# Another order of the attention stage's 100 steps per group

## The chip, the cores and the metric

One core of a Trainium2 chip runs the whole kernel. The metric is the device time of one launch in microseconds, as the median of several runs.

## What is computed

A macaron layer on x of 2 x 1024 x 256 in float32: half a feed-forward block, attention, half a feed-forward block again, each with a layer norm before it.

```
x = x + 0.5 * ffn(layernorm(x))     # silu(x Wg) * (x Wu), 2 of every 4 kept by size, times Wd; hidden 1024
x = x + attention(layernorm(x))     # 32 heads of 8, 8 heads of keys and values, rotary, causal, softmax
x = x + 0.5 * ffn(layernorm(x))
```

The change is in the attention alone:

```
scores = q k^T / sqrt(8), masked above the diagonal      # 1024 x 1024 for each head
attn   = softmax(scores)                                 # with the row's maximum taken off first
out    = attn v, then out Wo + bo
```

## The kernel before

The kernel has four phases: feed-forward, the projections to q, k and v, attention, feed-forward. Each engine has its own program, and semaphores tie them together. The attention works through 16 **groups**: 2 sequences times 8 key heads, with the 4 query heads that share a key head. The maximum of each row of scores is needed before the exponentials. So the scores are computed twice: once with queries on the partitions, for the maxima (`maximum_scores`, L1325), and once with keys on the partitions, for the exponentials (`s_head`, L1354). In the second, the maxima are taken off by rows that are added to q.

Per group there are four kinds of steps, and TensorE, ScalarE and GpSimd all take them in the order of one string, `ORDER`:

- **m**, 48 of them: one matmul of 64 rows, 128, 256, 384 or 512 columns wide, into one of four banks (`m_ps`). VectorE takes the maximum of each (L1418 with the causal mask, L1421 without), in the same sequence. The first 32 m's of the string are of the second half of the next group's rows, the last 16 of the first half of the group after. They alternate wide and narrow: m0 to m7 are 512 and 128 columns, m8 to m15 512 and 256, m16 to m23 512 and 384, m24 to m32 all 512, then m33 128 and m34 512, and on to m39 128 and 512 in turns, m40 to m47 384 and 256. After m31 VectorE joins the maxima of the two halves of the keys (L1436).
- **s**, 40 of them: one head of a unit of scores, into one of three banks (`s_ps`). ScalarE takes the exponential (L1471) into one of five buffers (`probs`). A unit is four heads. The string's s's run two units ahead of its v's. s's take their operands from partitions 0 to 63, m's from 64 to 127 (`s_lane`, `m_lane`).
- **t**, 2 of them: four transposes of the split maxima of 512 rows, into a bank of `m_ps` (`turn_shift`, L1333). ScalarE copies it out (L1477), and SP loads it by four DMAs into q (L1594). GpSimd makes the split (L1533, L1535) from VectorE's maxima.
- **v**, 10 of them: one unit of probabilities times values, for four heads, into one bank (`o_ps`, L1370). Units 0, 3 to 7 are 512 columns wide, 1 and 8 are 256, 2 and 9 are a piece of 384 and one of 128. Units 0, 1, 2 and 7, 8, 9 lie on the diagonal, and GpSimd masks them first (L1510). After v2 and v9 ScalarE copies the bank out (L1484), and v3 and the next v0 wait for that.

An m waits for VectorE to be done with the user of its bank, an s for the exponential three heads back, a v for the exponentials and masks of its unit. Banks of m's and t's are dealt in turns along the order:

```
RING = first_steps + [step for g in range(GROUPS) for step in steps(g) if step[0] in "mt"]
BANK = {step: i % M_BANKS for i, step in enumerate(RING)}
BANK_USER = dict(zip(RING[M_BANKS:], RING))
```

VectorE has other work in some groups: in groups 10 and 14 four reciprocals each (L1078), between m's. In groups 14 and 15 the m's run out.

Of the kernel before, what the change touches and what calls it, by code (L numbers as in the profile page):

```python
# [1164 lines left out]
def attention_programs(nc, ctx, group_rows, v, region, s_ps, m_ps, o_ps, output, normed, ident_bf, x, bo_row, T, HD, earlier):  # L1165
# [23 lines left out]
    for qc in range(QC):  # L1189
# [31 lines left out]

    ORDER = ("msmssmvsmmmsmsvsmmsmtmsmmmssmsmvs"
             "mmmssmsmvsmsmmsvmssmmsvmsmsmsvmsm"
             "ssmmsssmvssmmmtmsvmmmssmsmvmsmssmm")
    FIRST_MAXIMA = 16
    FIRST_TURNS = (26, 11)
    LEAD_IN = 1
    FIRST_HEADS = (AHEAD + LEAD_IN) * QPK  # L1230
    assert [ORDER.count(kind) for kind in "smtv"] == [SU * QPK, MU, QC, SU]

    def steps(g):

        count = dict.fromkeys("smtv", 0)
        for kind in ORDER:
            n = count[kind]
# [430 lines left out]
def build(nc, x_in, w_qkv, bias_cols, bv, w_o, bo, w_gate, w_up, w_down, cos_t, sin_t, out, HD=8, SPLIT=4):  # L1668
# [7 lines left out]
    with ExitStack() as ctx:  # L1676
# [55 lines left out]
        for b in range(BLKS):  # L1732
# [24 lines left out]
        late = Region(nc, late_at)  # L1757
        output = Output(nc, ctx, late, hole, x, w_o.rearrange("(k p) n -> p k n", p=P), inverse_rows, KVH, C // HD // KVH, HD, T, N, out_ps)
        attention, before_groups, first_scores, first_maxima, hooks = attention_programs(
            nc, ctx, group_rows, v, att_region, s_ps, m_ps, o_ps, output, normed2, ident_bf, x, bo, T, HD, earlier)  # L1760
        between["fills"] += [lambda pool: group_rows.fill_q(pool, 0),
# [55 lines left out]
```

## Time and profile before

| | |
|---|---|
| median of 3 runs | 829.38 us (826.87 to 832.43) |
| the profiled execution | 832.21 us |
| its span | 830.7 us |
| TensorE busy | 774.4 us, 93% |
| VectorE busy | 721.2 us, 87% |
| ScalarE busy | 491.5 us, 59% |
| GpSimd busy | 262.3 us, 32% |
| attention's groups | from about 250 to 680 us |

Times in the rows are microseconds from the start of the span. The profile shows when each instruction ran on its engine, and the idle time before it in brackets with what ended it. Instructions of one line that follow each other are merged into one row, with their number behind an x; the time is that of all of them. TensorE's ends are modelled. PEclk is the share of TensorE's full clock that was granted.

### The profile page before, as it was taken

To read this page: it belongs to the slowest core of one execution; us is meant where nothing else is said; L and a number is where in the kernel's file an instruction comes from. 1 tells how busy PE (TensorE), PEld (TensorE's weight loads), DVE (VectorE), ACT (ScalarE), POOL (GpSimd) and SP (SyncE) were. 2 spreads that over 40 slices of the span, in tenths; PEclk is the share of its full clock that TensorE was granted. 3 is DMA by queue.
4 is the path that set the end of the run, shared out by engine and by line. 5 is a ranking of instruction groups with operands and counts; after the bars stand their busy time and mean duration, and the time that the engine had idled before them with its cause. 6 is when DMAs were issued, how large, how long until landed. Compare 5 with 4: busy or idle time off the path is not lost.

```text
span 830.7 us, 15658 instructions
## 1 busy us (share of the span) xinstructions
PE 774.4 (93%) x5168; PEld 508.7 (61%) x5168; DVE 721.2 (87%) x1862; ACT 491.5 (59%) x949; POOL 262.3 (32%) x359
## 2 busy tenths in 40 slices
PE   4999999989899999999999989999899999999996
PEld 3787887977654544444444444444444468888886
DVE  3989999986797999999999989999987259999997
ACT  6444443311135888888888868888678734443441
POOL 1143533058720332322322222155315210534330
PEclk9999999999857999999999989999999999999999
DMA  8100000026913321233311332533313000000001
GB/s 294 53 0 2 0 1 1 1 107 173 297 33 69 71 66 37 61 74 72 70 41 39 72 70 54 132 67 76 72 21 85 15 8 1 1 26 1 26 2 51
DMA packets 21968, 48.62 MB, mean 59 GB/s; under 512 B 3744, under 2 KB 8224, under 8 KB 21376
## 3 DMA queue, kind: packets, MB, share of 16 engines
q1 hardware_dynamic: 21824, 47.56, 21.9%
q8 instruction: 41, 0.67, 0.4%
q14 instruction: 39, 0.32, 0.1%
q10 hardware_dynamic: 64, 0.07, 0.0%
HBM read 19.63 MB, written 14.16 MB: 41 GB/s over the span
## 4 chain that ended last, share of the span: by engine, by line
PE 61%; DVE 20%; issue 8%; POOL 5%; ACT 5%; DMA 1%; PEldq 0%; DVEq 0%; PEld 0%; SPq 0%; ACTq 0%; POOLq 0%
PE att_o_ps L1370 17%; PE att_m_ps L1325 15%; PE att_s_ps L1354 10%; PE ffn_gate L218 5%; PE ffn_up L218 5%; PE ffn_y_ps L351 5%; DVE ffn_hs L524 2%; DVE ffn_h L566 2%; POOL qkv_turned L859 2%; POOL qkv_parts L864 2%; ACT att_probs L1471 2%; DVE att_maxima L1421 2%; DVE att_scratch L1418 1%; DVE ffn_rank L510 1%; DVE ffn_pair_max L498 1%
## 5 line engine op out<-in xcount | busy, mean ns | idle before, releaser
L1471 ACT ACTIVATE att_probs<-att_s_ps 128x512 f32<-128x512 f32 (+1 forms) x640 | 314.3, 558 | 92.4 <-PE att_s_ps L1354 90.4
L1325 PE MATMUL att_m_ps<-k,q 64*128 64x512 f32 (+3 forms) x768 | 240.9, 413 | 15.5 <-DVE att_maxima L1418 13.6
L1418 DVE CUSTOM_DVE_ANT_0 att_scratch<-att_m_ps,att_causal 128x512 bf16<-128x512 f32 (+3 forms) x512 | 234.3, 485 | 20.9 <-PE att_m_ps L1325 17.9
L1354 PE MATMUL att_s_ps<-q,k 64*128 64x512 f32 (+3 forms) x768 | 223.3, 392 | 3.9 <-ACT att_probs L1471 3.9
L1325 PEld LDWEIGHTS att_m_ps<-k,q 64*128 64x128 f32 x768 | 132.9, 196 | 105.2 <-DVE att_maxima L1418 57.4
L1421 DVE TENSOR_REDUCE att_maxima<-att_m_ps 128x1 f32<-128x512 f32 x256 | 175.9, 687 | 11.5 <-PE att_m_ps L1325 11.3
L1370 PE MATMUL att_o_ps<-att_probs,att_vs 128*32 128x512 f32 (+3 forms) x1536 | 161.4, 508 | 1.6 <-POOL att_probs L1510 1.6
L1510 POOL TENSOR_SCALAR_AFFINE_SELECT att_probs<-att_probs 128x512 f32<-128x512 f32 x128 | 79.9, 637 | 262.3 <-ACT att_probs L1471 262.3
L1354 PEld LDWEIGHTS att_s_ps<-q,k 64*128 64x128 f32 x768 | 122.5, 190 | 64.8 <-ACT att_probs L1471 62.0
L630 POOL TENSOR_TENSOR ffn_hs_lo<-ffn_hs,ffn_hs_hi 128x512 fp32r<-128x512 f32 x48 | 76.6, 1621 | 106.4 <-ACT ffn_hs_hi L427 106.4
L454 ACT ACTIVATE ffn_a<-ffn_h 128x512 f32<-128x512 f32 x64 | 40.5, 633 | 106.8 <-DVE ffn_h L566 106.8
L351 PE MATMUL ffn_y_ps<-wd_hi,ffn_hs_hi 128*128 128x256 f32 x256 | 73.8, 288 | 6.2 <-DVE x L554 2.7
L351 PE MATMUL ffn_y_ps<-wd_lo,ffn_hs_hi 128*128 128x256 f32 x256 | 73.0, 285 | 0.0
L351 PE MATMUL ffn_y_ps<-wd_hi,ffn_hs_lo 128*128 128x256 f32 x256 | 72.9, 285 | 0.0
L1370 PEld LDWEIGHTS att_o_ps<-att_probs,att_vs 128*32 128x32 f32 x1536 | 34.1, 110 | 56.4 <-issue 41.8
L566 DVE TENSOR_TENSOR ffn_h<-ffn_up,ffn_silu 128x512 f32<-128x512 f32 x64 | 43.6, 682 | 23.0 <-ACT ffn_silu L449 22.0
L218 PE MATMUL ffn_gate<-ffn_xt_hi,wg_hi 128*128 128x512 f32 x128 | 52.2, 408 | 3.6 <-DVE ffn_h L566 1.6
L351 PEld LDWEIGHTS ffn_y_ps<-wd_hi,ffn_hs_hi 128*128 128x128 f32 x256 | 49.4, 193 | 9.4 <-DVE x L554 2.9
L218 PE MATMUL ffn_gate<-ffn_xt_lo,wg_hi 128*128 128x512 f32 x128 | 50.8, 397 | 0.9 <-DVE ffn_xt_lo L199 0.9
L427 ACT ACTIVATE ffn_hs_hi<-ffn_hs 128x512 fp32r<-128x512 f32 x56 | 35.0, 632 | 27.0 <-DVE ffn_hs L524 27.0
L218 PE MATMUL ffn_gate<-ffn_xt_hi,wg_lo 128*128 128x512 f32 x128 | 50.9, 398 | 0.0
L218 PE MATMUL ffn_up<-ffn_xt_lo,wu_hi 128*128 128x512 f32 x128 | 50.7, 396 | 0.0
(114 smaller groups left out, 1166.8 us busy)
## 6 DMA issues: line engine op xcount, KB each, us to landing
q_rows<-qkv_parts SPq DMA_DIRECT2D x16, 512.0 KB, 4.6
q<-q_rows SPq DMA_DIRECT2D x16, 512.0 KB, 4.6
q<-q SPq DMA_DIRECT2D x16, 512.0 KB, 4.3
k_rows<-qkv_parts SPq DMA_DIRECT2D x8, 256.0 KB, 3.0
k<-k_rows SPq DMA_DIRECT2D x16, 128.0 KB, 5.2
k<-k SPq DMA_DIRECT2D x16, 128.0 KB, 4.3
q<-att_shift_t SPq DMA_DIRECT2D x128, 4.0 KB
out_num<-att_sums SPq DMA_DIRECT2D x128, 16.0 KB
```

Source lines behind the costliest of these rows:

```text
L218: last = pe.matmul(bank, w[w_part], xt[:, k, :], start=(k == 0 and n == 0), stop=(k == self.KT - 1 and n == 2))
L351: last = pe.matmul(y_ps[:, t, :], hp[:, blk, j, rows], wp[:, blk, j, :], start=(blk == 0 and j == 0 and m == 0 and t % 2 == 0), stop=(blk ...
L454: act.activation(a[:, blk, j, :], h[:, blk, j, :], ACT.Abs).then_inc(abs_ready, 1)
L566: dve.tensor_tensor(h[:, blk, j, :], gu[j % 2][1][:], silu[:, j % 2, :], ALU.mult).then_inc(h_ready, 1)
L630: pool.tensor_tensor(hs_lo[:, blk, j, :], hs[:, j, :], hs_hi[:, blk, j, :].bitcast(F32), ALU.subtract).then_inc(lo_ready, 1)
L1325: pe.matmul(m_ps[BANK["m", n]][:, :cols], q[g % 2][m_lane, h, t * P:(t + 1) * P], k[g % 2][m_lane, kc * N:kc * N + cols], start=True, stop ...
L1354: last = pe.matmul(s_ps[n % S_BANKS][:, at:at + w], k[g % 2][s_lane, kb * P:(kb + 1) * P], q[g % 2][s_lane, h, qc * N + q0:qc * N + q0 + w ...
L1370: last = pe.matmul(o_ps[32 * h:32 * (h + 1), q0:q0 + w], vs[g % 2][:, kb, :], probs[u % len(probs)][:, h, at:at + w], start=(u in CHUNK_FI ...
L1418: dve.tensor_tensor_reduce(out=scratch[bank][:, :n], in0=m_ps[bank][:, :n], in1=causal[:, N - n:], scale=1.0, scalar=LOWEST, op0=ALU.add, ...
L1421: dve.tensor_reduce(top_of, m_ps[bank][:, :n], mybir.AxisListType.X, ALU.max).then_inc(m_taken, 1)
L1471: act.activation(probs[u % len(probs)][:, h, SPAN[u]], s_ps[n % S_BANKS][:, SPAN[u]], ACT.Exp, scale=SCALE).then_inc(exp_done, 1)
L1510: pool.affine_select(out=blk, in_=blk, compare_op=ALU.is_ge, fill=0.0, base=0, pattern=[[0, QPK], [1, P]], channel_multiplier=-1).then_inc ...
```

## The change

Only the string `ORDER` changes. It has the same 100 letters in another sequence: 40 s, 48 m, 2 t, 10 v. All three engines that read it follow, and the banks are dealt anew along it.

```diff
-    ORDER = ("msmssmvsmmmsmsvsmmsmtmsmmmssmsmvs"
-             "mmmssmsmvsmsmmsvmssmmsvmsmsmsvmsm"
-             "ssmmsssmvssmmmtmsvmmmssmsmvmsmssmm")
+    ORDER = ("smsmmvmsmsmsmvsmmmssmsmmtssmsmvms"
+             "mssmmsmmvsmmssmvmsmsmsvmsmsmsvsms"
+             "smmmsssmvmsmsmsmmvtsmmmmmsssmvmsmsm")
```

Cut at the v's, with v0 ahead of the first cut and the string's end joined to its start, these are the stretches behind each v:

```
     before               after
v0   smmmsms              msmsmsm
v1   smmsmtmsmmmssmsm     smmmssmsmmtssmsm
v2   smmmssmsm            msmssmmsmm
v3   smsmms               smmssm
v4   mssmms               msmsms
v5   msmsms               msmsms
v6   msmssmmsssm          smssmmmsssm
v7   ssmmmtms             msmsmsmm
v8   mmmssmsm             tsmmmmmsssm
v9   msmssmmmsmssm        smsmsmsmm
```

## Rows read from the trace of the kernel before

**Rows 1.** Windows of one group; us, then each engine's busy time, clock, DMA.
```profile
408.34:433.82 25.48, 24.43 (x201) 12.08 (x200) 23.82 (x82) 21.31 (x45) 6.60 (x15) 1.00 0.28 63
486.22:515.23 29.01, 27.35 (x201) 12.93 (x200) 25.54 (x84) 21.19 (x45) 6.37 (x14) 0.88 0.19 41
593.85:622.86 29.01, 26.83 (x202) 13.15 (x201) 25.85 (x84) 21.31 (x45) 6.36 (x14) 0.88 0.20 41
```

**Rows 2.** VectorE's maxima by shape, six ordinary groups; busy us, mean ns.
```profile
L1421 DVE TENSOR_REDUCE att_maxima<-att_m_ps 128x1 f32<-128x512 f32 x97 | 66.7, 688 | 2.0 <-PE att_m_ps L1325 2.0
...
L1418 DVE CUSTOM_DVE_ANT_0 att_scratch<-att_m_ps,att_causal 128x384 bf16<-128x384 f32 x48 | 26.5, 553 | 2.6 <-PE att_m_ps L1325 2.3
...
L1418 DVE CUSTOM_DVE_ANT_0 att_scratch<-att_m_ps,att_causal 128x256 bf16<-128x256 f32 x48 | 20.0, 418 | 0.0
...
L1418 DVE CUSTOM_DVE_ANT_0 att_scratch<-att_m_ps,att_causal 128x128 bf16<-128x128 f32 x48 | 13.7, 286 | 5.3 <-PE att_m_ps L1325 4.6
```

**Rows 3.** VectorE's timeline, one ordinary group; start, length in us.
```profile
410.06 0.29 DVE L1418 CUSTOM_DVE_ANT_0 att_scratch<-att_m_ps,att_causal 128x128 bf16<-128x128 f32 x1 [0.45 <-PE att_m_ps L1325]
...
415.95 0.69 DVE L1421 TENSOR_REDUCE att_maxima<-att_m_ps 128x1 f32<-128x512 f32 x1 [0.17 <-PE att_m_ps L1325]
...
427.79 0.29 DVE L1418 CUSTOM_DVE_ANT_0 att_scratch<-att_m_ps,att_causal 128x128 bf16<-128x128 f32 x1 [0.33 <-PE att_m_ps L1325]
...
429.66 0.29 DVE L1418 CUSTOM_DVE_ANT_0 att_scratch<-att_m_ps,att_causal 128x128 bf16<-128x128 f32 x1
...
431.96 0.56 DVE L1418 CUSTOM_DVE_ANT_0 att_scratch<-att_m_ps,att_causal 128x384 bf16<-128x384 f32 x1 [0.33 <-PE att_m_ps L1325]
```

**Rows 4.** TensorE's timeline, the same group; ends are modelled.
```profile
410.28 0.64 PE L1370 MATMUL att_o_ps<-att_probs,att_vs 128*32 128x256 f32 x8
...
411.92 0.38 PE L1333 MATMUL att_m_ps<-ident_bf,att_shift 128*8 128x128 bf16 x4 [0.29 <-DVE att_maxima L1421]
...
412.23 0.49 PE L1325 MATMUL att_m_ps<-k,q 64*128 64x512 f32 x1
...
414.27 1.07 PE L1370 MATMUL att_o_ps<-att_probs,att_vs 128*32 128x384 f32 x16
...
417.12 1.06 PE L1370 MATMUL att_o_ps<-att_probs,att_vs 128*32 128x512 f32 x8
...
420.34 0.39 PE L1325 MATMUL att_m_ps<-k,q 64*128 64x512 f32 x1
...
420.57 0.39 PE L1325 MATMUL att_m_ps<-k,q 64*128 64x512 f32 x1
...
424.34 0.52 PE L1325 MATMUL att_m_ps<-k,q 64*128 64x512 f32 x2
...
425.78 1.07 PE L1370 MATMUL att_o_ps<-att_probs,att_vs 128*32 128x512 f32 x8
...
427.61 0.38 PE L1333 MATMUL att_m_ps<-ident_bf,att_shift 128*8 128x128 bf16 x4
...
428.14 0.49 PE L1325 MATMUL att_m_ps<-k,q 64*128 64x512 f32 x1 [0.15 <-DVE att_maxima L1418]
...
428.58 0.64 PE L1370 MATMUL att_o_ps<-att_probs,att_vs 128*32 128x256 f32 x8
...
429.15 0.33 PE L1325 MATMUL att_m_ps<-k,q 64*128 64x128 f32 x1
...
430.01 0.38 PE L1325 MATMUL att_m_ps<-k,q 64*128 64x256 f32 x1
...
430.33 1.07 PE L1370 MATMUL att_o_ps<-att_probs,att_vs 128*32 128x384 f32 x16
...
433.40 0.49 PE L1325 MATMUL att_m_ps<-k,q 64*128 64x512 f32 x1
```

**Rows 5.** Timelines of ScalarE and of SP's queue, the same group.
```profile
432.12 0.59 ACT L1484 ACTIVATE att_sums<-att_o_ps 128x512 f32<-128x512 f32 x1
...
429.04 2.40 SPq L1594 DMA_DIRECT2D q<-att_shift_t  x4
```

More of the change, by code:

```diff
@@ L1219, in attention_programs @@
     LAST = GROUPS - 1
-    ORDER = ("msmssmvsmmmsmsvsmmsmtmsmmmssmsmvs"
-             "mmmssmsmvsmsmmsvmssmmsvmsmsmsvmsm"
-             "ssmmsssmvssmmmtmsvmmmssmsmvmsmssmm")
+    ORDER = ("smsmmvmsmsmsmvsmmmssmsmmtssmsmvms"
+             "mssmmsmmvsmmssmvmsmsmsvmsmsmsvsms"
+             "smmmsssmvmsmsmsmmvtsmmmmmsssmvsmsm")
     FIRST_MAXIMA = 16
```

## The prediction

> **What bounds the kernel now.** I read the windows first, one per group of the attention stage, from a group's first value step to the next group's. An ordinary group lasts 25.48 us, and in it TensorE is busy 24.43, VectorE 23.82, ScalarE 21.31 [rows 1]. No engine is full and two nearly are. The change keeps every instruction and moves only places in a queue, so busy time stays and only idle time can go. Then I read VectorE's timeline: the gaps in rows 3 lie each at the first m behind a v. Last, TensorE's timeline, for what it was doing there.
>
> Names: m0 to m47, s0 to s39, T0, T1 and v0 to v9 are the letters of ORDER, counted by kind. v0 opens the window at 408.34 and the next v0 closes it at 433.82 [rows 1]; between them v1 is at 410.28, v2 414.27, v3 417.12, v7 425.78, v8 428.58, v9 430.33 [rows 4].
>
> **What the change leaves alone.** From v3 to v7 (8.66 us, [rows 4]) the new order has the same m's and s's between the same v's, some neighbours swapped: nothing. The last score of a unit stands 5 to 8 scores ahead of its v, as before, so exponentials and masks are in time. Nothing is added on POOL or SP. ScalarE's copy of the output bank behind v9 runs until 432.71, 2.38 us after v9 [rows 5]; my walk puts the next v0 2.72 after it, so it fits, by 0.3. T1 moves behind m39 and v8, and with it SP's four loads of the shift, issued in 2.40 us from 429.04, 1.43 after T1 at 427.61 [rows 4, 5]; next_m and store_sums stand behind them on SP, both early. s4 needs these loads. In my walk it comes 6.5 us after T1; 1.4 for the copy, 2.4 for the issue and 1.2 for the last landing (an estimate: half of the issue time) make 5.0. It fits by 1.5 us; each us beyond would cost a us per group.
>
> **The laws that I walk with.** (a) m's and T's share four banks in a ring. An m starts 0.07 after VectorE is done with the unit four places back (m38 at 428.14: m35 was started at 427.79 and took 0.29, [rows 3, 4]); a T in between counts as a place. (b) Units of 512, 384, 256 and 128 columns take 688, 553, 418 and 286 ns [rows 2]. 24 of the widest and 8 of each other make 26.6 us a group, 2.8 more than VectorE is busy [rows 1]: where there is no gap, a unit starts before the last one's end, by 2.8 over some 40 such places, 0.07; I take 0.08, so 0.61, 0.47, 0.34 and 0.20 from start to start. (c) What follows a v starts 0.07 before its end, 0.57 after v8 (m39 at 429.15), 1.0 after the longer ones. VectorE takes an m that is first behind a v 0.51 later (128 columns, m39, taken at 429.66) to 0.63 (384: v9 to m44, 1.63 in all), and one behind a score 0.1 to 0.2 later still (v0 to m3 1.72, v2 to m16 1.68) [rows 3, 4]. (d) From the last m to the v it is 0.42 (m2, 433.40), or 0.32 if that m is 256 wide (m43, 430.01) [rows 4].
>
> **The walk**, v7 as zero. Today s31 and s32 stand between v7 and m35; VectorE gets m35 2.01 after v7, having ended m34 0.33 before [rows 3]. In the new order m35 is first and VectorE takes it as soon as it can, 0.33 + 0.08 earlier, at 1.60.
> **v7 to v8**: m36 to m39 are taken at 1.80, 2.41, 2.61, 3.22. m39 waits for m35's bank (1.96), so v8 is at 2.20.
> **v8 to v9**: T1 at 2.77; T0 to m10 took 0.31 (411.92, 412.23, [rows 4]), so m40 starts at 3.08 and reaches VectorE at 3.71, which was free at 3.42. m41 is taken at 4.18 and done at 4.60, which gives m45 its bank at 4.67; v9 at 5.00. The units go on to 6.14.
> **v9 to v0**: s38 first, so m46 reaches VectorE at 5.00 + 1.68 = 6.68. m2 needs its bank: 6.68 + 0.55 + 0.07 = 7.30, v0 at 7.72.
> **v0 to v1**: m3 first, taken at 9.23; VectorE was free at 8.91. There are nine weights to load here for today's eight, so 2.05 for 1.94 and v1 at 9.77.
> **v1 to v2**: m7 stands behind s5 and comes at 11.05, 0.2 late. From there VectorE sets the pace, 0.20 + 0.61 + 0.34 + 0.61 to m11 at 12.81, done 13.23. And here the new order loses: T0 stands between m12 and m13, no longer between m9 and m10, so m14, the last m before v2, has m11's bank: m14 at 13.30, v2 at 13.72. Only m12 to m14 are left as cover from 13.15 on, 0.61 + 0.34 + 0.61, to 14.71. m15, 256 wide, comes at 13.72 + 1.57 = 15.29: VectorE waits 0.5 where it waited 0.17 [rows 3].
> **v2 to v3**: m16 is taken at 15.63, done at 16.32; m20 gets its bank, v3 at 16.81. With 8.66 more the next v7 is at 25.47.
>
> | from, to | today | new |
> |---|---|---|
> | v7, v8 | 2.80 | 2.20 |
> | v8, v9 | 1.75 | 2.80 |
> | v9, v0 | 3.49 | 2.72 |
> | v0, v1 | 1.94 | 2.05 |
> | v1, v2 | 3.99 | 3.95 |
> | v2, v3 | 2.85 | 3.09 |
> | v3, v7 | 8.66 | 8.66 |
> | sum | 25.48 | 25.47 |
>
> So the order trades: it takes away the wait at v7 (0.4), and gives it back, 0.34 at v2 and the rest at T1. Of 16 groups the last has no m's and the one before 32 of 48, some 14.5 periods: 0.01 x 14.5, nothing. The profiled execution took 832.2 and would take 832.1; it lies 2.8 above the median of the runs, which stays at **829**.
>
> **Bounds.** No row has a T straight behind a v. If it costs nothing there, m40 starts at 2.77 and VectorE hardly waits: 0.28 off the period. If it costs twice T0's price it is 0.3 on top. I take T0's 0.31, the only price of a T in a row. m15 lies between 0.51 and 0.64 behind its v; I take 0.57. v0 to v1 is at least today's 1.94. An error of 0.05 in (c) counts at four v's. Together some 0.4 either way per group, 6 us. The clock adds: two groups with reciprocals on VectorE last 29.01 us, at a granted clock of 0.88; VectorE is 1.72 to 2.03 busier in them than in the ordinary one, which leaves 1.8 in the first that the low clock explains, and 1.5 in the second [rows 1]. They may come or go: 3 us.
>
> **A rule to weigh.** Two m's in a row, 512 and 128 wide, take 0.52 together (424.34): less the 0.28 of the second, it starts 0.24 after the first. Where m's alternate with s's, one m follows the other after 0.23 (420.34, 420.57) [rows 4]. So neighbours of one kind cost TensorE next to nothing. The Trainium skill (TensorE: Matmul & The Clock Gate, Part 3, "The mechanism") says that a weight load overlaps a running matmul only when it is for other rows of the array, which an m and an s are and two m's are not. By it each pair of neighbours of one kind would pay a load; 26 pairs in the old string and 23 in the new, by that page's columns over 1.2 GHz 0.107 us each (an estimate), make 0.3 a group, and the sum 825. The row speaks against it.
>
> **The rivals.**
> *The cover is longer than I walk* (faster). If m14 starts earlier than (a) says, v2 costs no more than today (0.34 less per group) and m7 isn't late (0.2): 0.54 x 14.5 is 8 us, 821; if T1 is free behind v8 as well, 12 us, 817. For it: the gap at v7 is surely gone, and the gain stays if nothing else grows. Against: (a) gives m38 to 0.01. Chance 0.22.
> *The clock falls in ordinary groups* (slower). At v2 and v9 TensorE sits still a little longer than now, and the granted clock has fallen over whole groups, those with the longest waits [rows 1]. A group so hit costs 1.8 (the first of them). From five of fourteen on the kernel is slower by 1%; with seven it is 842, with all 854. Against: ordinary groups show 1.00, and a new wait is 0.3 longer at most. Chance 0.08.
> *The shift lands too late for s4* (slower). It needs 1.5 us of error in my walk, and 2.1 for 1%. Chance 0.04.
> *What the order is built on is fixed.* From a v to what follows is 1.0 us whatever follows, so an order can't shorten it, only cover it. That ends where my forecast ends.
>
> **How the numbers follow.** Forecast, with that last one, 0.66; longer cover 0.22; clock 0.08; shift 0.04. 1% (8.3 us) is about what a measurement of this kernel can tell from no change. The forecast's bounds put 0.02 over the edge on the slow side; of the longer cover 0.02 stays within 1%. Faster 0.20, within 1% 0.66, slower 0.14. The range goes down to the middle of the longer cover, 819, and up by the 6 and a part of the clock's 3, to 837.
>
> **What would show it.** VectorE without a gap at m35; gaps, ends to starts, of about 0.2 at m40, 0.45 at m46, 0.25 at m3, 0.1 at m7 and 0.5 at m15; v8 to v9 longer by 1 us, v2 to v3 by 0.2; an ordinary group of 25.5. No gap at m15 would mean that (a) is wrong about T0's place, and a gain. A granted clock below 1.00 in an ordinary group, or s4 waiting for a DMA, would make me wrong on the other side.

## The result and the profile after

| | before | changed |
|---|---|---|
| median of 20 runs each, us | 830.35 | 834.22 |
| lowest and highest run | 826.32, 839.99 | 828.74, 836.06 |
| profiled execution, us | 832.21 | 834.75 |
| its span, mean granted clock | 830.7, 0.965 | 833.2, 0.961 |

The ratio is 1.004, with a 95% interval of 1.0022 to 1.0058. Ratios compare runs of both kernels that were made together, and leave out the few that lie over 1.5% above the fastest run of their kernel. The time is inside the range and inside 1%, but it is not "no change": the new order costs 3 to 4 us, and by the interval at least 1.8. Of the distance from the forecast, 829, to 834.22, 1.0 us is the kernel before itself, 829.38 by the three runs known at the forecast and 830.35 by all 20.

Busy time of VectorE (723.3 us for 721.2) and ScalarE (489.9 for 491.5) did not move much, as it should with the same instructions. TensorE's did, 783.2 for 774.4: its matmuls overlap less, 24.91 us for 24.43 in an ordinary group at full clock, and more of them ran at half clock. This is the page's granted clock of the changed kernel, 40 slices of 20.8 us each, in tenths:

```profile
PEclk9999999999956999999999989999999799999999
```

Three dips are there: the start of the attention stage (slices 12 and 13), a group with reciprocals on VectorE (24), and slice 32, from 645.7 on. The kernel before has the first two and stands at 9 in slice 32. (The reciprocals' groups 10 and 14 are counted as VectorE does, which works ahead. In time the eight reciprocals of before lie in groups 8 and 9, at 480.5 to 491.8, and in 12 and 13, at 587.6 to 598.7.)

**Ordinary groups went as walked.** TensorE's timeline of the changed kernel, one ordinary group, its v's and T's:

```profile
401.13 1.07 PE L1370 MATMUL att_o_ps<-att_probs,att_vs 128*32 128x512 f32 x8
...
403.51 0.64 PE L1370 MATMUL att_o_ps<-att_probs,att_vs 128*32 128x256 f32 x8
403.96 0.39 PE L1333 MATMUL att_m_ps<-ident_bf,att_shift 128*8 128x128 bf16 x4
...
406.28 1.07 PE L1370 MATMUL att_o_ps<-att_probs,att_vs 128*32 128x384 f32 x16
...
408.97 1.06 PE L1370 MATMUL att_o_ps<-att_probs,att_vs 128*32 128x512 f32 x8
410.96 0.64 PE L1370 MATMUL att_o_ps<-att_probs,att_vs 128*32 128x256 f32 x8
...
413.64 0.39 PE L1333 MATMUL att_m_ps<-ident_bf,att_shift 128*8 128x128 bf16 x4
...
414.92 1.07 PE L1370 MATMUL att_o_ps<-att_probs,att_vs 128*32 128x384 f32 x16
...
418.00 1.06 PE L1370 MATMUL att_o_ps<-att_probs,att_vs 128*32 128x512 f32 x8
...
426.51 1.07 PE L1370 MATMUL att_o_ps<-att_probs,att_vs 128*32 128x512 f32 x8
```

From start to start, against the column "new" of the walk: v7 (401.13) to v8 2.38 for 2.20; v8 to v9 2.77 for 2.80; v9 to v0 2.69 for 2.72; v0 to v1 1.99 for 2.05; v1 to v2 3.96 for 3.95; v2 to v3 3.08 for 3.09; v3 to v7 8.51 for 8.66. [rows 4] has the v's of before; the largest changes are v8 to v9, 1.75 then and 2.77 now, and v9 to v0, 3.49 then and 2.69 now.

VectorE's timeline of the changed kernel, the waits in one such period; the bracket is the idle time ahead of a unit:

```profile
405.00 0.56 DVE L1418 CUSTOM_DVE_ANT_0 att_scratch<-att_m_ps,att_causal 128x384 bf16<-128x384 f32 x1 [0.18 <-PE att_m_ps L1325]
...
407.92 0.56 DVE L1418 CUSTOM_DVE_ANT_0 att_scratch<-att_m_ps,att_causal 128x384 bf16<-128x384 f32 x1 [0.36 <-PE att_m_ps L1325]
...
410.48 0.29 DVE L1418 CUSTOM_DVE_ANT_0 att_scratch<-att_m_ps,att_causal 128x128 bf16<-128x128 f32 x1 [0.23 <-PE att_m_ps L1325]
...
416.50 0.42 DVE L1418 CUSTOM_DVE_ANT_0 att_scratch<-att_m_ps,att_causal 128x256 bf16<-128x256 f32 x1 [0.52 <-PE att_m_ps L1325]
...
421.53 0.69 DVE L1421 TENSOR_REDUCE att_maxima<-att_m_ps 128x1 f32<-128x512 f32 x1 [0.17 <-PE att_m_ps L1325]
```

These are m40, m46, m3, m15 and m24, forecast 0.2, 0.45, 0.25, 0.5 and nothing; m35's gap of 0.33 [rows 3] is gone. The wait behind v2 is the one that grew: it was 0.17 there, ahead of m16 [rows 3], and is 0.52 now, ahead of m15. m24's wait is not new: the kernel before has 0.17 there too, at 420.65.

The windows of the changed kernel: two groups of the kind of [rows 1], and then six windows of 4 us behind them, in group 14, where the maxima run out (columns as in [rows 1]: length, then TensorE, its weight loads, VectorE, ScalarE, POOL, and the granted clock).

```profile
408.97:434.35 25.38, 24.91 (x202) 12.35 (x201) 23.79 (x82) 21.20 (x45) 6.67 (x14) 1.00 0.29 63
485.99:514.73 28.74, 27.56 (x202) 13.61 (x201) 25.46 (x84) 21.16 (x45) 6.38 (x14) 0.88 0.20 43
634.00:638.00 4.00, 3.88 (x31) 1.59 (x27) 3.33 (x9) 3.53 (x9) 1.70 (x4) 1.00 0.11 22
638.00:642.00 4.00, 3.16 (x28) 1.89 (x28) 0.00 (x0) 3.58 (x8) 1.22 (x2) 0.98 0.07 12
642.00:646.00 4.00, 4.00 (x26) 2.02 (x22) 0.00 (x0) 2.20 (x7) 1.06 (x2) 0.50 0.01 4
646.00:650.00 4.00, 4.00 (x21) 1.55 (x13) 0.00 (x0) 2.12 (x4) 0.81 (x3) 0.50 0.13 24
650.00:654.00 4.00, 3.78 (x20) 3.01 (x16) 0.69 (x1) 0.90 (x2) 1.32 (x3) 0.74 0.05 11
654.00:658.00 4.00, 4.00 (x22) 1.53 (x21) 0.00 (x0) 2.64 (x6) 0.00 (x0) 0.68 0.02 4
```

The same stretch of the kernel before:

```profile
638.00:642.00 4.00, 3.73 (x26) 1.91 (x22) 2.42 (x7) 3.02 (x9) 1.65 (x4) 1.00 0.13 25
642.00:646.00 4.00, 3.84 (x36) 1.85 (x35) 0.00 (x0) 3.42 (x8) 1.85 (x3) 1.00 0.03 7
646.00:650.00 4.00, 3.49 (x24) 1.77 (x26) 0.00 (x0) 3.45 (x9) 0.63 (x1) 1.00 0.07 14
```

An ordinary group lasts 25.38 at full clock. At 641.8 the clock falls from 1.00 to 0.50 (2.4 to 1.2 GHz), stays there for 10.2 us, and is at 0.50 again for 3.4 us from 655.5; the kernel before keeps 1.00. What TensorE did just before is in the timeline of the changed kernel (all engines, only the rows that matter):

```profile
639.02 0.64 PE L1370 MATMUL att_o_ps<-att_probs,att_vs 128*32 128x256 f32 x8
...
639.48 0.39 PE L1333 MATMUL att_m_ps<-ident_bf,att_shift 128*8 128x128 bf16 x4
...
639.80 0.84 PE L1354 MATMUL att_s_ps<-q,k 64*128 64x512 f32 x3
...
640.22 0.59 ACT L1477 ACTIVATE att_shift_t<-att_m_ps 8x512 fp32r<-8x512 bf16 x1
...
641.48 0.38 PE L1354 MATMUL att_s_ps<-q,k 64*128 64x256 f32 x1 [0.84 <-ACT att_probs L1471]
...
641.79 1.93 PE L1370 MATMUL att_o_ps<-att_probs,att_vs 128*32 128x384 f32 x16
```

v8 and T1 go out, then the scores s34 to s37 with no m between them. ScalarE puts T1's copy (640.22) among the exponentials, so s37 finds no free score bank and TensorE sits still for 0.84 us; 0.3 us later the clock is half, and v9 at 641.79 takes 1.93 where it takes 1.07 in an ordinary group (406.28). In an ordinary group m's fill that place. The runs show how regular this is: 17 of the 20 have a mean clock of 0.957 to 0.963, and three have 0.967 and take 829.4 on the mean, so the fall comes in most executions and not in all.

**Where the 2.5 us between the two profiled executions came from.** Up to the first v of group 1 the changed kernel is later by 1.31 us (281.68 for 280.37). Its groups 1 to 13 take 337.84 for 342.49, 4.65 less, of which 1.85 is one group that had 6.8 us of half clock before ([rows 1], 593.85) and has none now. From the start of group 14 to the start of the last v it is 58.32 for 52.37, 5.95 more. 1.31 - 4.65 + 5.95 = 2.6. So it isn't a change that does nothing: two effects stand against each other. How much of the 4.65 is the order and how much the clock comes below.

### The profile page after: what moved, and what is told of

It is laid out like the page before. It is cut to its first block, busy times and chain, and to the rows that moved or that the text cites. A ratio compares the mean times of both kernels' runs of the same rounds, so it can differ in the third digit from the quotient of the medians.

```text
span 833.2 us, 15658 instructions
## 1 busy us (share of the span) xinstructions
PE 783.2 (94%) x5168; PEld 515.0 (62%) x5168; DVE 723.3 (87%) x1862; ACT 489.9 (59%) x949; POOL 263.3 (32%) x359
## 4 chain that ended last, share of the span: by engine, by line
PE 62%; DVE 19%; issue 6%; POOL 5%; ACT 5%; DMA 1%; PEldq 0%; PEld 0%; DVEq 0%; SPq 0%; ACTq 0%; POOLq 0%
PE att_o_ps L1370 18%; PE att_m_ps L1325 15%; PE att_s_ps L1354 11%; PE ffn_gate L218 5%; PE ffn_up L218 5%; PE ffn_y_ps L351 5%; DVE ffn_h L566 2%; DVE ffn_hs L524 2%; ACT att_probs L1471 2%; POOL qkv_turned L859 2%; DVE att_maxima L1421 2%; POOL qkv_parts L864 2%; PE out_y_ps L1152 1%; DVE ffn_xn L181 1%; DVE ffn_rank L510 1%
## 5 line engine op out<-in xcount | busy, mean ns | idle before, releaser
L1325 PE MATMUL att_m_ps<-k,q 64*128 64x512 f32 (+3 forms) x768 | 248.3, 414 | 7.3 <-DVE att_maxima L1418 5.3
L1354 PE MATMUL att_s_ps<-q,k 64*128 64x512 f32 (+3 forms) x768 | 217.6, 389 | 6.0 <-ACT att_probs L1471 5.0
L351 PEld LDWEIGHTS ffn_y_ps<-wd_lo,ffn_hs_hi 128*128 128x128 f32 x256 | 49.7, 194 | 1.5
L218 PE MATMUL ffn_up<-ffn_xt_hi,wu_hi 128*128 128x512 f32 x128 | 50.5, 395 | 0.0
```

The source lines that it names most:

```text
L218: last = pe.matmul(bank, w[w_part], xt[:, k, :], start=(k == 0 and n == 0), stop=(k == self.KT - 1 and n == 2))
L351: last = pe.matmul(y_ps[:, t, :], hp[:, blk, j, rows], wp[:, blk, j, :], start=(blk == 0 and j == 0 and m == 0 and t % 2 == 0), stop=(blk ...
L1325: pe.matmul(m_ps[BANK["m", n]][:, :cols], q[g % 2][m_lane, h, t * P:(t + 1) * P], k[g % 2][m_lane, kc * N:kc * N + cols], start=True, stop ...
L1354: last = pe.matmul(s_ps[n % S_BANKS][:, at:at + w], k[g % 2][s_lane, kb * P:(kb + 1) * P], q[g % 2][s_lane, h, qc * N + q0:qc * N + q0 + w ...
```

## The experiments

OLD and NEW stand for the two strings in all cuts of code here. Three kernels are built on the kernel before (e2, the one with the new tail; e8, with NEW in group 0 alone; e11, with fillers), the others on the changed one; `order_of(g)` takes ORDER's place in `steps(g)`, so the string may differ by group.

**First, where is the loss?** Two kernels put the strings together by group:

```
+    def order_of(g):
+        return OLD if g >= 14 else NEW      # e1
+        return NEW if g >= 14 else OLD      # e2
```

> The new order in groups 0 to 13, the old one in groups 14 and 15. Theory A (the ordinary groups gain a little, 4.6 us by group 14 in the traces, and the change loses 5.9 us behind it, as TensorE's clock falls once the m's have run out in group 14 and T1 stands behind v8): about 4 us faster than before, ratio 0.995, granted clock 1.00 from 640 to 660 us. Theory B (the change loses in the ordinary groups or around them, the tail is chance): about the time of the changed kernel, ratio 1.004.

Measured: 829.6 us, ratio 0.9998 (0.9974 to 1.0023), 4.6 us under the changed kernel by the medians and 3.5 by the ratios. The clock stays at 1.00 from 640 to 660; it falls once behind that, for 3.4 us at 670.7.

> The old order in groups 0 to 13, the new one in 14 and 15. Theory A: the loss stands alone, 5 to 6 us slower than before, ratio 1.006, clock at half for about 14 us behind 640 us. Theory B: as before, 1.000.

Measured: 835.6 us, ratio 1.0055 (1.0028 to 1.0081). Its windows:

```profile
638.00:642.00 4.00, 4.00 (x33) 2.17 (x31) 0.90 (x4) 3.51 (x8) 2.13 (x5) 1.00 0.10 18
642.00:646.00 4.00, 3.17 (x22) 1.69 (x21) 0.00 (x0) 2.29 (x7) 0.79 (x2) 0.69 0.01 4
646.00:650.00 4.00, 4.00 (x17) 1.99 (x16) 0.00 (x0) 2.28 (x6) 0.63 (x1) 0.50 0.08 15
650.00:654.00 4.00, 4.00 (x22) 2.75 (x21) 0.00 (x0) 1.28 (x3) 1.92 (x3) 0.53 0.10 20
```

and TensorE's timeline of the same kernel, the one wait there:

```profile
643.03 0.38 PE L1361 MATMUL att_s_ps<-q,k 64*128 64x256 f32 x1 [0.83 <-ACT att_probs L1478]
```

The same wait to 0.01 us and the same fall behind it, 10.2 and then 3.4 us long. The loss is in the last two groups, whole: with the new tail alone it is 835.6, and without it the new order is level with the old one. It is not 0.995, though, as I had expected from groups 1 to 13; that stays for below.

**Is it the clock, or the waits themselves?** The next kernel keeps NEW in all groups and gives TensorE work that nobody needs in group 14: where m35 to m47 stood, 13 matmuls of 64x512 into a bank that nobody reads (`[...]` stands for indices left out).

```
+            elif fill and g == LAST - 1 and kind == "m" and count["m"] > 35:
+                yield "f", count["m"] - 1
+        def filler(first):
+            if first:
+                pe.wait_ge(m_taken, GROUPS * MU)
+            pe.matmul(m_ps[...], q[LAST % 2][...], k[LAST % 2][...], start=True, stop=True)
```

> The changed kernel with 13 matmuls of 64x512 more in group 14, in the places of m35 to m47, which have no work there; their results are used by nobody. If it is the low clock that costs the 6 us, and TensorE's lack of work that makes it fall: faster than the changed kernel by 4 to 6 us though it does more, ratio to before 0.996. If the loss is of waits in the new sequence: no faster, or slower by the 1 to 2 us that the extra matmuls take.

Measured: 829.8 us, ratio 0.9993 (0.997 to 1.0015). Its windows of the same stretch:

```profile
638.00:642.00 4.00, 4.00 (x44) 2.37 (x44) 0.00 (x0) 3.12 (x8) 1.83 (x3) 1.00 0.03 7
642.00:646.00 4.00, 3.84 (x32) 1.97 (x29) 0.00 (x0) 3.63 (x8) 0.89 (x2) 1.00 0.07 13
```

It does more work than the changed kernel and takes 4.4 us less, with an interval below that kernel's (1.0022 to 1.0058), and the clock stays at 1.00. A theory of waits alone can't give that: the order of the needed steps is the same, and they come no sooner for the extra matmuls. From v7 to s37 it is 4.48 us here (635.66, 640.14) and 4.40 in the changed kernel (637.08, 641.48), where the clock is still 1.00. It is the clock.

The same fillers in the kernel before, where the clock doesn't fall:

> The kernel before with the 13 extra matmuls in group 14. The old order keeps the clock up there in its profiled run, so the theory that extra work helps only where the clock falls gives 1.000, or 0.998 if some of before's slower runs come of it. If the extra matmuls helped the changed kernel by another way, as by shifting later waits, they help here too: 0.994.

Measured: 832.54 us, ratio 1.0017 (0.999 to 1.0044). Group 14 takes 25.47 for 24.99. So the fillers cost 0.5 us themselves, and the gain above comes from what they prevent.

**Is it T1's place?** NEW everywhere, but in groups 14 and 15 T1 goes out ahead of v8 instead of behind it (`...mmvts...` becomes `...mmtvs...`).

> The changed kernel, with T1 ahead of v8 in groups 14 and 15 alone. If it is T1 behind v8 (ScalarE copies it while s37 waits for an exponential, 0.84 us idle just before the clock falls) that sets the clock off: ratio to before about 0.996, clock 1.00 behind 640 us. If it is the sequence of the rest of group 14: 1.004 as the changed kernel.

Measured: 833.34 us (827.73 to 839.02), ratio 1.0027 (0.9996 to 1.0057). The profiled execution (828.59) has no fall there, at a mean clock of 0.968; but the median of its runs' clocks is 0.963, and seven of the twelve take 833 us or more. So it is no cure, and no test of T1's place either, since the wait that it was to remove is still there. These are the same two windows and the same wait in the profiled execution:

```profile
638.00:642.00 4.00, 3.15 (x28) 1.53 (x30) 0.00 (x0) 3.75 (x8) 1.57 (x3) 1.00 0.05 11
642.00:646.00 4.00, 3.84 (x35) 2.06 (x31) 0.00 (x0) 2.88 (x8) 0.93 (x2) 1.00 0.05 11
```

```profile
641.06 0.38 PE L1361 MATMUL att_s_ps<-q,k 64*128 64x256 f32 x1 [0.85 <-ACT att_probs L1478]
```

TensorE waits 0.85 us ahead of s37, in a window where it is busy for 3.15 us, as in the changed kernel (0.84 and 3.16), and the clock stays at 1.00. So a stretch like this one can lose the clock and need not, and what decides between the two isn't shown. It also gives the price of the fall with nearly the same order: from the start of group 14 to the start of the last v it is 52.59 us here, 58.32 in the changed kernel.

**Group 14 or group 15?** NEW except in group 14:

```
+        return OLD if g == 14 else NEW
```

> The new order everywhere but in group 14. If group 14 sets the clock off, in which TensorE runs out of m's, the tail is as with the old order: 1.000 to before, no low clock from 640 to 660 us. If it is group 15 (no m's at all), the low stretch stays, nearer to 655 us, and the ratio is 1.003 or more.

Measured: 830.88 us, ratio 0.9999 (0.9962 to 1.0036). The long fall is gone. One of 3.4 us is left, at 651.2, in group 15, which has NEW; from the start of group 14 to the last v it is 54.18 us, between the 52.39 of the kernel with the old tail (e1) and the 58.32 of the changed one. Group 14, whose m's run out behind two thirds, is the place of the long fall.

**The one new wait of ordinary groups.** I had put the wait of 0.52 at m15 down to T0 behind m12. This kernel moves T0 alone, in groups 0 to 13 (OLD in 14 and 15):

```
-    ORDER = ("smsmmvmsmsmsmvsmmmssmsmmtssmsmvms"
+    ORDER = ("smsmmvmsmsmsmvsmmmtssmsmmssmsmvms"
```

> New order in groups 0 to 13 with T0 moved back from behind m12 to behind m9, old order in 14 and 15. My theory of the step v1 to v3: T0 takes one of the last four places of the bank ring before v2, so m14 starts one unit later and VectorE waits 0.5 us for m15. With T0 moved, v1 to v2 goes from 3.95 to 3.6, VectorE's gap at m15 from 0.5 to 0.2, the ordinary group from 25.4 to 25.05, the time to 0.994 of before. The rival, that the gap at m15 comes of m15 standing behind v2 and not ahead of it: the gap stays, the group stays at 25.4, the ratio at 1.000.

Measured: 832.38 us, ratio 1.0008 (0.9976 to 1.0041). TensorE's timeline of that kernel, v1, T0 and v2:

```profile
411.29 0.64 PE L1377 MATMUL att_o_ps<-att_probs,att_vs 128*32 128x256 f32 x8
...
412.70 0.38 PE L1340 MATMUL att_m_ps<-ident_bf,att_shift 128*8 128x128 bf16 x4
...
415.19 0.49 PE L1332 MATMUL att_m_ps<-k,q 64*128 64x512 f32 x1
415.62 1.07 PE L1377 MATMUL att_o_ps<-att_probs,att_vs 128*32 128x384 f32 x16
```

and VectorE's, m15:

```profile
417.19 0.42 DVE L1425 CUSTOM_DVE_ANT_0 att_scratch<-att_m_ps,att_causal 128x256 bf16<-128x256 f32 x1 [0.63 <-PE att_m_ps L1332]
```

My theory fell. v1 to v2 grew to 4.33 where I had expected it to shrink, the wait at m15 is 0.63, longer than the 0.52 that it was to remove, and the ordinary group lasts 25.77 for 25.39, where the rival had it unchanged. T0 has to wait for the bank of an earlier m at its new place (it starts 1.41 after v1), and s6 behind it starts 1.72 after v1, where it was 0.91 in the changed kernel. The exponentials then start late, and s9, s10 and s11 each wait for one of them (they start 2.94, 3.42 and 3.90 us after v1, each 0.05 behind the end of an exponential). m14 stands behind s11 in the queue, so it starts with it at 3.90, and v2 0.43 after it. In the changed kernel m14 starts at 3.53, right when m11 gives up its bank. So at v2 two limits lie close together, the ring of banks and ScalarE's exponentials, and my explanation by the ring alone was half of it: in the changed kernel m14 starts when the ring lets it, and with T0 moved the exponentials are later than that.

**The other end: group 0.** The first v of group 1 was 1.3 us later in the changed kernel. One kernel has OLD in groups 0, 14 and 15, one has NEW in group 0 alone:

```
+        return OLD if g in (0, 14, 15) else NEW      # e7
+        return NEW if g == 0 else OLD                # e8
```

> The old order in groups 0, 14 and 15, the new one between. The traces with the new order show 1.0 to 1.6 us more from the first m to the first v of group 1, and the clock at half for 41 us there where most with the old one have 37.6. If that is of group 0's order: the first v of group 1 comes 63.8 to 64.5 us after the first m (65.4 with the new order), and the ratio to before is 0.996. If it is chance: 65.4, and 1.000 as with the old tail alone.

Measured: 829.13 us (826.74 to 832.12), ratio 0.9964 (0.9929 to 0.9999).

> The counterpart: the new order in group 0 alone. If group 0 costs: 65.4 us from the first m to group 1, 1.0 to 1.5 us slower than before, ratio 1.0015. If chance: 64, and 1.000.

Measured: 831.05 us, ratio 0.9988 (0.9948 to 1.0027).

The time from the first m to v0 of group 1, in the profiles of all kernels:

```
OLD in group 0   64.47  63.82  63.33  65.11  65.08  65.08
NEW in group 0   64.90  65.47  65.42  65.36  65.42  65.34  65.62
```

Most of this is the half clock at the stage's start, which lasts 34.1, 37.5 or 41.0 us with OLD and 37.5 or 41.0 with NEW. OLD itself spans 1.8 us, more than the strings lie apart. Where the half clock lasted 41.0 us, OLD has 65.08 and 65.11, and NEW 65.34 to 65.47: a cost of NEW in group 0 is some 0.3 us there, and whether it also lengthens the half clock isn't shown.

**Can fillers help more?** The e7 kernel with the 13 fillers in group 14, and with 16 small matmuls instead, one behind each of the last 16 m's ahead of the first v:

```
+            if heads and n >= MU:
+                pe.matmul(o_ps[:, :P], q[1][m_lane, 0, :P], k[1][m_lane, :P], start=True, stop=True)
```

> The best so far, the old order in groups 0, 14 and 15 and the new one between, with the 13 extra matmuls in group 14. With the old order there the clock fell late only at times, so the extra work should give little: 0.996 to before, as without it. If the low clock behind 640 us happens in a part of the old tail's runs too: 0.994, and no run above 832.

Measured: 830.62 us, ratio 0.9997 (0.9977 to 1.0017).

> The same orders without those, and with 16 extra matmuls of 64x128 ahead of group 0, one behind each of the last 16 m's before the first value step, where the clock is at half; their results are used by nobody. If TensorE's lack of work there holds the clock down: it rises one or two steps of 3.4 us sooner, and group 1 starts 0.5 to 2 us sooner, 61.5 to 63 us after the first m (63.3 without). If not, they cost up to 0.1 us each: 63.3 to 65.

Measured: 831.81 us, ratio 1.0018 (1.0000 to 1.0037), group 1 65.08 us behind the first m. Misses, both: no gain shows where the clock holds anyway or stays half anyway. The medians are 1.5 and 2.7 us above e7's, but e9's interval overlaps e7's, so that the fillers cost anything there isn't shown for it.

**What is left: why the good versions are level and not faster.** Each run has its granted clock, so runs can be compared at the same clock. The runs that the ratios use, mean time and number:

| mean granted clock | kernel before | NEW, OLD in 14 and 15 | changed |
|---|---|---|---|
| 0.961 | | | 834.1 (10) |
| 0.967 | 831.8 (19) | 829.3 (7) | 829.4 (3) |
| 0.969 to 0.971 | 830.6 (28) | 829.2 (1) | |
| median of the runs' clocks | 0.971 | 0.967 | 0.961 |

At one clock the new order is faster by 2.5 us (831.8 - 829.3), if half clock costs the same wherever it lies. The traces give the same without that condition. A group that ran wholly at full clock can be compared between the profiles with OLD in it (the kernel before, e2, e8, e11) and with NEW. It is 0.26 longer in group 1, 0.1 shorter in each of five, 0.2 in each of 3 and 10, 0.46 in 4, 0.6 in each of 8 and 12, the same in 9 (26.51 and 26.52), and in the changed kernel 0.1 shorter in 13: 2.5 together. So of the 4.65 us above some 2.5 are the order, and the other 2.2 are clock: the kernel before had 13.7 us of half clock in these groups, and the changed one 6.8.

But the new order's runs have a lower clock by 0.004 in the median even with the old tail, which is 0.004 x 830 x 2 = 6.6 us more at half clock. The 13.7 us of it in the tail cost about 5, so 6.6 would cost some 2.4 (an estimate); by group 9, which lasts 27.44 in e1 with 3.4 us of half clock and 26.52 without, 1.8. That is most of the gain or all of it. Where the runs lose it no view shows: falls of 3.4 us lie around 490, 590 and 672 in many profiles of either order, and they come and go from run to run. In groups 1 to 13 they add up to 0 to 13.7 us in the four profiles with OLD and to 3.4 to 10.2 in the eight with NEW. e7, at 0.969, is the only one whose interval lies below 1, just; e9 differs from it by fillers and is at 0.9997. A version that beats both kernels isn't established.

## Why the forecast was off

**The walk held.** 25.47 forecast, 25.38 measured; no stretch is off by more than 0.18. Gaps came where they were walked to, with their sizes to 0.1. Two differences are real: v6 to v7 is 0.15 shorter than before (it lies in "v3 to v7: nothing"), because m34 starts 2.41 us after v6 for 2.56; and v7 to v8 gives the same back, since VectorE reaches m35 1.75 after v7 and not 1.60. m24's gap of 0.17 I had not listed; it stands in the kernel before as well.

**The laws.** (a), the ring of four banks, put m14 where it was. (c) and (d), the distances at a v, held to 0.1. T straight behind a v, the operation without a row, cost its 0.3: m40 is taken with a wait of 0.18 for the 0.2 forecast. The shift and the output copy were in time, as the walk had them; no s4 waited for a DMA.

**A rule to weigh.** With three neighbours of one kind fewer, the rule of the Trainium skill (TensorE: Matmul & The Clock Gate, Part 3, "The mechanism") gave 825, by 0.3 us a group. The ordinary group moved by 0.1, so a gain of that size isn't there. But my row did not speak against the rule as I said. It set m's in a row, 0.24 apart, against alternating ones, 0.23 apart; but there an s starts together with each m (both at 420.57), two matmuls in the time of one. And the changed kernel has a pair further apart: m38 and m39 take 0.56 together (403.02), of which the second is 0.22, so they start 0.34 apart. What a pair costs TensorE these runs don't settle.

**The step that failed** is the sentence "Of 16 groups the last has no m's and the one before 32 of 48, some 14.5 periods: 0.01 x 14.5, nothing." It holds two errors.

First, it counts groups 14 and 15 as parts of an ordinary group and doesn't walk them. There the m's are missing, VectorE is idle, and TensorE's queue is what is left of the string: in NEW, v8, T1 and four scores in a row with nothing to fill, and ScalarE's copy for T1 among their exponentials. That gives the wait of 0.84 us, and behind it, in most executions, the half clock of 10.2 + 3.4 us. Its price by the medians is 4.6 us between the changed kernel and the one with the old tail, and 5.0 between the kernel before (830.62 beside these runs) and the one with the new tail; by the ratios it is 3.5 and 4.6. OLD has scores and v's mixed there, its longest wait in the stretch is 0.27 us, and the clock stays up. That the group loses the clock is shown. That the wait by itself sets it off is not: the same wait in e4's profile is followed by full clock.

Second, "0.01" was mis-sized. Groups 1 to 13 gained 4.65 us in the profiled executions: +0.2 in group 1, -0.1 in each of five ordinary groups, -0.2 and -0.45 in groups 3 and 4, -0.6 in each of 8 and 12, -0.3 in each of 9 and 10, and -1.85 in 13, which is nearly all clock (-0.1 without it). At equal clock the gain is 2.5 us, by the runs and by the groups at full clock, where the sum had 0.15. I had walked one group of the 13 and took the unusual ones as its equals; 2.1 of the 2.5 come from groups 3, 4, 8, 10 and 12.

The clock was among my rivals, with the right kind of loss (TensorE sits still longer, the granted clock falls) and the wrong place: "in ordinary groups", where it stayed at 1.00. I had priced it from 1% on, five groups and more, and had no case for a fall in one group of the tail, 4 to 5 us. Nor did it fall "over whole groups" in [rows 1], but for 6.8 of the 29 us in each of the two. At full clock those two groups last 26.51 and 27.27 (e8), so the low clock cost 2.5 and 1.7 us in them, where I had 1.8 and 1.5. That the median came out within 1% is in part luck: a loss of 4 to 5 us in the tail, a gain of 2.5 at equal clock and its loss again by a lower clock, and none of the three was in the sum.

## What to carry to other kernels

A schedule that was found for the steady period must be walked through its first and last periods too, above all through the one where one kind of work runs out: what filled a place there no longer does. Look at the granted clock in those windows, and in more than one execution: a wait of under a microsecond on TensorE was followed by 10 us of half clock in two profiles here, and by none in a third. When two versions are level, compare their runs at equal clock before concluding that the change did nothing: here a gain of 2.5 us and a loss of 4 to 5 were both real.

## What was not expected of the hardware

- After a wait of 0.84 us on TensorE, in a window where it was busy 3.16 of 4 us, the clock went to half for 10.2 us; e2 did the same behind 0.83. The same wait in e4 (0.85, busy 3.15 of 4 us), and shorter ones in the kernel before (0.27, at 639.3), had no such effect. What decides isn't settled by these runs.
- 13 matmuls whose result nobody reads made the kernel faster by 4.4 us where the clock would mostly have fallen, and group 14 slower by 0.5 where it wouldn't.
- The start of the attention stage ran at half clock for 34.1 to 41.0 us in every profile, whatever the order, though TensorE was busy for 36.69 of those 37.50 us in the kernel before (223.9 to 261.4); 16 small matmuls more there did not end it sooner (37.5 us in e10; 34.1 in e7, the same kernel without them).
